# Conv block with a binarized two-layer FFN on one core: another band-load layout, the residual on VectorE, and fp16 parts split over three engines

## The reference

```python
w_sym = (w + rot90(w,1) + rot90(w,2) + rot90(w,3)) * 0.25      # 192 kernels of 7x7
x = x + depthwise_conv(layernorm_over_channels(x), w_sym, pad=3)
t = tokens(x)                                                  # (16, 1024, 192)
h = quant(layernorm(t) @ sign(W1 - mean).T + b1)               # 5 groups along the batch and along the weights' rows
o = quant(gelu(h) @ sign(W2 - mean).T + b2)                    # quant(y) = clip(y * 128 / (max|y| + 1e-5))
x = from_tokens(t + o)
```

## Time and profile before

| | us |
|---|---|
| median of 3 runs | 747.52 |
| the profiled execution | 749.42 |
| its span | 747.5 |

### The profile page before, as it was taken

One profiled execution on the slowest core, in us unless ns is written; L12 is line 12 of the kernel. 1 busy time (PEld: TensorE's weight loads), 2 busy tenths in 40 slices (PEclk: granted clock), 3 DMA queues, 4 the chain that ended last, 5 costly groups with the idle time before them and its releaser, 6 DMA issues.

```text
span 747.5 us, 9920 instructions
## 1 busy us (share of the span) xinstructions
PE 567.7 (76%) x3618; PEld 378.9 (51%) x3618; DVE 481.8 (64%) x1082; ACT 425.7 (57%) x666; POOL 13.7 (2%) x27
## 2 busy tenths in 40 slices
PE   4443379999449798365677888889898898989964
PEld 3443268888348687232233444445455454545543
DVE  1979501010002656859889677799999999988752
ACT  3689600000000040144489887899999999999910
POOL 3001000000000000000000000000000000000000
PEclk9878599999759899578899998999999999999985
DMA  7985167777537474980001010022212131213455
GB/s 184 312 183 139 45 154 180 185 191 169 128 92 181 119 178 103 354 300 0 2 21 43 22 42 22 1 63 65 80 48 85 64 128 65 84 57 114 143 165 157
DMA packets 92438, 87.20 MB, mean 117 GB/s; under 512 B 10153, under 2 KB 75689, under 8 KB 92390
## 3 DMA queue, kind: packets, MB, share of 16 engines
q1 hardware_dynamic: 57040, 69.66, 32.3%
q10 hardware_dynamic: 35350, 16.92, 9.2%
HBM read 62.55 MB, written 23.99 MB: 116 GB/s over the span
## 4 chain that ended last, share of the span: by engine, by line
PE 39%; ACT 25%; DVE 13%; issue 11%; DMA 7%; ACTq 3%; SPq 1%; POOL 0%; POOLq 0%; DVEq 0%
PE bank L876 16%; ACT arena L499 8%; ACT arena L493 6%; PE bank L947 6%; PE bank L865 5%; ACT arena L507 4%; DMA arena<-x 3%; DMA arena<-kz_d 3%; DVE ST L606 2%; ACT arena L516 2%; PE bank L926 2%; ACT arena L479 2%; PE bank L928 2%; PE bank L927 2%; PE bank L912 2%
## 5 line engine op out<-in xcount | busy, mean ns | idle before, releaser
L876 PEld LDWEIGHTS bank<-arena 128*128 128x128 f32 x1152 | 141.7, 199 | 51.4 <-DMA arena<-kz_d 30.1
L876 PE MATMUL bank<-arena 128*128 128x112 f32 (+1 forms) x1152 | 142.3, 282 | 25.1 <-DMA arena<-kz_d 25.1
L493 ACT ACTIVATE arena<-bank,b1s 128x512 f32<-128x512 f32 x180 | 125.4, 700 | 60.7 <-PE bank L928 60.3
L947 PE MATMUL bank<-arena 128*128 128x512 f32 (+1 forms) x360 | 123.5, 440 | 35.4 <-ACT arena L516 35.4
L672 DVE COPY arena<-bank 128x512 f32<-128x512 f32 x24 | 16.6, 691 | 163.5 <-PE bank L876 163.4
L432 ACT ACTIVATE arena<-bank 128x512 f32<-128x512 f32 x24 | 14.3, 595 | 178.9 <-PE bank L876 162.0
L756 DVE TENSOR_TENSOR arena<-arena 128x1024 f16<-128x1024 f32 (+1 forms) x60 | 98.8, 1659 | 24.4 <-ACT arena L507 24.3
L761 DVE TENSOR_REDUCE am<-arena 128x1 f32<-128x3072 f32 x30 | 100.2, 3340 | 0.5 <-ACT arena L493 0.5
L499 ACT ACTIVATE arena<-arena,gm 128x1024 f32<-128x1024 f32 x90 | 100.5, 1167 | 0.0
L926 PE MATMUL bank<-arena 128*128 128x512 f16 x180 | 71.9, 399 | 36.0 <-DVE arena L751 13.9
L507 ACT ACTIVATE arena<-arena 128x1024 f16<-128x1024 f32 (+1 forms) x90 | 82.8, 929 | 0.9 <-PE bank L957 0.9
(11 more groups left out here) (115 smaller groups left out, 657.4 us busy)
## 6 DMA issues: line engine op xcount, KB each, us to landing
arena<-park_d SPq DMA_DIRECT2D x44, 384.0 KB, 3.5
arena<-kz_d SPq DMA_DIRECT2D x96, 96.0 KB, 3.0
arena<-kz_d ACTq DMA_DIRECT2D x96, 96.0 KB, 2.8
park_d<-arena SPq DMA_DIRECT2D x6, 1536.0 KB, 15.0
arena<-x SPq DMA_DIRECT2D x8, 1024.0 KB, 9.5
out<-arena SPq DMA_DIRECT2D x32, 256.0 KB, 2.0
arena<-kz_d SPq DMA_DIRECT2D x96, 64.0 KB, 2.5
arena<-kz_d ACTq DMA_DIRECT2D x96, 64.0 KB, 3.0
```

The lines of the kernel that those rows point to most:

```text
L493: act.activation(yslot(s)[:, 2 * m:2 * m + 2, :], m1p[c % 2][:, :].rearrange("p (h n) -> p h n", h=2), ACT.Identity, bias=b1s[:, m:m + 1], ...
L876: last = t.matmul(ps[:, :, lo:hi], WB[BUFS[u]][:, 1 - db, e, :], xn[:, :, lo + db:hi + db], start=False, stop=(c == CG - 1 and db == -1))
L947: last = t.matmul(o, wt[:, 0:P], src, start=(m == n == 0), stop=(m == MT - 1 and n == 1))
```

## The change

The band table gets another form. `KX[channel pair half, column w, channel, kernel row, w']` is built with 32 copies, stored in four pieces (two DMAs each, interleaved with the third and fourth pair's loads), and read in units of four channels with runs of 896 bytes, all on SP's queue. A buffer holds for each channel 12 blocks of 32 columns, of which seven are written and the rest stay at the zeros that GpSimd writes once; there are two buffers, from unit 3 on three, from unit 24 on four. The rows of a block are in natural order, so `perm` and `by_rows` go. The residual is added by VectorE, which evicts all 48 groups. In the FFN `W2F` goes; all six blocks are fp16 high and low parts. ScalarE makes the high parts of blocks 0 to 2, VectorE those of blocks 3 to 5 in one copy, GpSimd all low parts in six instructions of 512 columns. From step 6 on `normal` and the new `high` stand first in VectorE's step.

```diff
-CG, CU = 4, 2
+CG = 4
+NQ = 3 * RB
+WW = CG * NQ * W
+KW = CG // 2 * KS * W
+KP = 8
-FIRST = 12
-BUFS = [u % 4 if u < FIRST else (4, 5, 0, 1, 2, 3)[(u - FIRST) % 6] for u in range(NCU)]
+THIRD, FOURTH = 3, 24
+BUFS = [(0, 1, 0)[u] if u < THIRD else (2, 1, 0)[(u - THIRD) % 3] if u < FOURTH else (3, 2, 1, 0)[(u - FOURTH) % 4]
+        for u in range(NCG)]
...
+                if k in (2, 3):
+                    for i in range(2 * (k - 2), 2 * (k - 1)):
+                        sp.wait_ge(ker_step, 8 + KP * (i + 1))
+                        for h in range(2):
+                            sp.dma_start(kz_d[:, KP * i:KP * (i + 1), h * KW:(h + 1) * KW],
+                                         KX[h * NCG:(h + 1) * NCG, KP * i:KP * (i + 1)].rearrange("p w s a u -> p w (s a u)")) \
+                                .then_inc(st_ker[i], 16)
+            def load_bands(u):
+                for r in range(RB):
+                    dst = WF[BUFS[u]][r * W:(r + 1) * W].rearrange("p (c q) -> p c q", c=CG)
+                    sp.dma_start(dst[:, :, (r + 1) * W:(r + 1 + KS) * W], kz_d[u].rearrange("w (c q) -> w c q", c=CG)) \
+                        .then_inc(ld_wb[BUFS[u]], 16)
+            for u in range(NCG):
+                sp.wait_ge(blank, 1 if u < THIRD else 2 if u < FOURTH else 3)
+                if user_before(u) >= 0:
+                    sp.wait_ge(conv, user_before(u) + 1)
+                load_bands(u)
...
+            pool.memset(view(R, 2 * WW), 0.0).then_inc(blank, 1)
+            pool.wait_ge(conv, THIRD)
+            pool.memset(WF[2], 0.0).then_inc(blank, 1)
+            pool.wait_ge(conv, FOURTH - 1)
+            pool.memset(WF[3], 0.0).then_inc(blank, 1)
+            def low(u, m0, done):
+                pool.wait_ge(done, u + 1)
+                for m in range(m0, m0 + half):
+                    last = pool.tensor_tensor(out=low_half(u, m, m + 1), in0=yslot(u)[:, 2 * m:2 * m + 2, :],
+                                              in1=hib(u, m, m + 1), op=ALU.subtract)
+                last.then_inc(lo2, 1)
             for s in range(FT + LAGF):
+                if 0 <= s - LAGH < FT:
+                    low(s - LAGH, half, hiV)
                 if 1 <= s <= FT and s % GT == 0:
                     g = s // GT - 1
                     pool.wait_ge(gmx, g + 1)
                     pool.partition_all_reduce(gm[:, 1:2], gm[:, 0:1], P, RMAX).then_inc(gall, 1)
+                if 0 <= s - LAGH < FT:
+                    low(s - LAGH, 0, hiA)
...
-                    if m in (0, 1, 3) and 0 <= k < FT:
-                        high(k, min(m, 2))
+                    if m < 2 and 0 <= k < FT:
+                        high(k, 2 * m, m + 2)
-                    if m >= 4 and 0 <= u < FT:
-                        gelus(u, m - 4)
+                    if m >= 3 and 0 <= u < FT:
+                        gelus(u, m - 3)
-                if 0 <= u < FT:
-                    gelus(u, 2)
...
             for g in range(NCG):
-                if g % 2:
-                    dve.wait_ge(conv, 2 * (g + 1))
-                    dst, src = conv_out_parts(g)
-                    v.tensor_copy(dst, src).then_inc(cev[1], 1)
+                dve.wait_ge(conv, g + 1)
+                dst, src = conv_out_parts(g)
+                v.tensor_tensor(out=dst, in0=src, in1=dst, op=ALU.add).then_inc(cev, 1)
...
+            def high(u):
+                dve.wait_ge(gelu, 3 * (u + 1))
+                if u >= 2:
+                    dve.wait_ge(mm2[1], u - 1)
+                v.tensor_copy(hib(u, MT // 2, MT), yslot(u)[:, MT:2 * MT, :]).then_inc(hiV, 1)
...
+                if s > 5 and s + 2 < FT:
+                    normal(s + 2)
+                if 0 <= s - LAGH < FT:
+                    high(s - LAGH)
...
-                if 0 <= s - LAGH < FT:
-                    low(s - LAGH, 0)
-                if 0 <= s - LAGH < FT:
-                    low(s - LAGH, 1)
...
             def conv_group(g):
                 if g >= 4:
-                    pe.wait_ge(cev[g % 2], (g - 4) // 2 + 1)
-                dst, src = cps[g % 4], X1[:, :, g * CG:(g + 1) * CG]
-                t.matmul(dst[:, :].rearrange("p (c n) -> p n c", c=CG), perm, src, start=True, stop=False)
+                    pe.wait_ge(cev, g - 3)
+                pe.wait_ge(ld_wb[BUFS[g]], 16 * RB * uses(g))
...
             def products(u, m):
-                if m < MF:
-                    return ((W2F, yslot(u)[:, 2 * m:2 * m + 2, :]),)
-                return ((W2T[:, m, :], hib(u, m, m + 1)), (W2T[:, m, :], low_half(u, m, m + 1)))
+                return hib(u, m, m + 1), low_half(u, m, m + 1)
             def lower(u, m):
                 if m == 0:
-                    pe.wait_ge(gelu, 3 * u + 1)
+                    pe.wait_ge(lo2, 2 * u + 2)
```

More of the change, by code:

```diff
@@ L43 @@
 OW = HALF + QTR
-WTN = (3 * HID + MT * C) // 2 + C
-PREP = 15
+WTN = (3 * HID + MT * C) // 2
+PREP = 14
 ARENA = 52544
@@ L240, in var1, with unit_pieces @@
             return VR[:, 2 * NB * (k % 3):2 * NB * (k % 3 + 1)]
[L242 to L247, removed]
+        KER_STEPS = 8 + W + 1
+        def unit_pieces(k):
+            return [i for i in range(W // KP) if i * KP * KW < (k - 1) * 2 * NB * C and (i + 1) * KP * KW > (k - 2) * 2 * NB * C]
         def batch_of(i):
@@ L499, in gelus, with high @@
                 act.activation(y, y, ACT.Gelu, scale=gm[:, 5:6]).then_inc(gelu, 1)
-            def high(u, part):
-                if part == 0 and u >= 2:
+            def high(u, m0, m1):
+                act.wait_ge(gelu, 3 * (u + 1))
+                if u >= 2:
                     act.wait_ge(mm2[1], u - 1)
-                act.wait_ge(gelu, 3 * u + part + 1)
-                m0, m1 = max(MF, 2 * part), 2 * part + 2
-                act.activation(hib(u, m0, m1), yslot(u)[:, 2 * m0:2 * m1, :], ACT.Copy).then_inc(hi2, 1)
+                last = act.activation(hib(u, m0, m1), yslot(u)[:, 2 * m0:2 * m1, :], ACT.Copy)
+                if m1 == MT // 2:
+                    last.then_inc(hiA, 1)
             def result(u, part):
@@ L875, in conv_group @@
                         lo, hi = max(0, -db), min(NB, NB - db)
-                        last = t.matmul(ps[:, :, lo:hi], WB[BUFS[u]][:, 1 - db, e, :], xn[:, :, lo + db:hi + db],
-                                        start=False, stop=(c == CG - 1 and db == -1))
-                    if e == CU - 1:
-                        last.then_inc(conv, 1)
+                        last = t.matmul(ps[:, :, lo:hi], WB[BUFS[g]][:, 1 - db, c, :], xn[:, :, lo + db:hi + db],
+                                        start=(db == 0), stop=(db == -1))
+                last.then_inc(conv, 1)
             for g in range(NCG):
@@ L930, in products @@
             def products(u, m):
[L932 to L934 removed]
+                return hib(u, m, m + 1), low_half(u, m, m + 1)
             def lower(u, m):
                 if m == 0:
[L938 removed]
+                    pe.wait_ge(lo2, 2 * u + 2)
                     if u >= 1:
                         pe.wait_ge(ev2, 2 * u - 1)
[L941 to L944 removed]
                 o = m2a[:, :].rearrange("p (h n) -> p h n", h=2)
[L946 to L947 removed]
+                for n, src in enumerate(products(u, m)):
+                    last = t.matmul(o, W2T[:, m, 0:P], src, start=(m == n == 0), stop=(m == MT - 1 and n == 1))
                 if m == MT - 1:
@@ L954, in upper @@
                 for m in range(MT):
-                    for n, (wt, src) in enumerate(products(u, m)):
+                    for n, src in enumerate(products(u, m)):
                         for e in range(2):
-                            last = t.matmul(m2b[e * C1:(e + 1) * C1, 0:QTR], wt[:, P:C], src[:, e, :],
+                            last = t.matmul(m2b[e * C1:(e + 1) * C1, 0:QTR], W2T[:, m, P:C], src[:, e, :],
                                             start=(m == n == 0), stop=(m == MT - 1 and n == 1))
                 last.then_inc(mm2[1], 1)
-            for e in range(2):
-                pe.wait_ge(cev[e], NCG // 2)
+            pe.wait_ge(cev, NCG)
             for s in range(-2, FT + LAGF):
```

178 lines of the change are left out of this document (57 added, 121 removed).

## The result

The changed kernel takes 779.12 us (median of 4 runs, 777.88 to 781.07) against 748.11 (747.02 to 748.77) for the kernel before: ratio 1.0418, 95% interval 1.0392 to 1.0445. It is slower, where 696 and faster were forecast, and it lies outside the range. The profiled execution took 777.88 with a span of 776.1.

What follows compares the result with a forecast made beforehand. TensorE's band products and permutation were taken to bound the convolution, a chain through ScalarE the FFN. Start +9, convolution -43 and FFN -17 on 749.4 gave 698.4, less 1.9: 696 us; range 662 to 735.

Steps and rivals of the forecast that it cites:

- The start, +9: Start: storing the larger band table delays the later pairs' loads and moves its end by 9 us, bounds 0 and 16.
- The permutation, -42, and bands and evictions that keep up: Convolution: dropping 48 permutations of 0.87 us saves 42 us; groups then take 2.67 us, with loads and evictions fast enough.
- rival B: Convolution: band loads from one queue take 3.3 us per unit and bound it, 723 us in all; chance 0.15.
- The first six groups: Convolution's beginning: with two buffers groups 0 to 5 end near 27 us after the start instead of 16, +11 us.
- Weight loads, +8 with bounds 0 and 20: Convolution: weight loads share some engines with the band loads and slow them, costing 8 us.
- group 24's wait: Convolution: unit 24 waits for its buffer's memset behind group 22, +4 us.
- Weight sums, +7: Convolution, behind group 35: TensorE waits for VectorE's eviction, statistics and weight sums and restarts slowly, +7 us.
- FFN steps of 10.5 us: FFN: steps fall from 11.92 to 10.5 us, with ScalarE as the chain.
- One GpSimd subtraction, 1.3 us: FFN: each 512-column GpSimd subtraction takes 1.3 us, bounds 0.5 and 2.8; six make 7.8 us per step.
- rival A: FFN: GpSimd is the bound, a subtraction taking 1.9 us or more; at 2.0 the kernel takes 766 us; chance 0.08.
- The order in GpSimd's queue costs at each group's end: FFN group ends: the all-reduce stands behind three subtractions, so ScalarE's gelus wait about 2.5 us for the scale, three times.
- The tail, +12 and +3: Tail: eight steps go from 6.46 to 8.0 us, bound by GpSimd, +12 us; the group's end adds +3.

Runs made afterwards that it cites:

- e7: e6 with each of the ten weight loads cut in two (48 + 3 and 32 + 6 partitions): 695.8 us.
- e11: e7 with the weight sums cut into five pairs, one behind each of groups 32 to 36: 689.4 us.
- e1: The changed kernel with a 128x1 GpSimd addition in place of each of the ten all-reduces: 696.7 us, one run.
- e5: The kernel before, with 25 small GpSimd operations of several kinds on scratch memory in its idle stretch under the convolution: 749.9 us.
- e3: The kernel before, with one 128x8 GpSimd subtraction on scratch memory ahead of each of the ten waits for the maxima: 751.4 us, one run.
- e6: The changed kernel with the maxima over partitions made by TensorE and VectorE, their broadcasts placed earlier in TensorE's order: 706.1 us.
- e8: e6 with the ten weight loads uncut but issued two at a time, behind groups 24, 26, 28, 30 and 32: 703.4 us.
- e9: The changed kernel with low parts on VectorE, weight loads cut as in e7, and the high copies of pieces 3 to 5 on GpSimd: 697.3 us.

## Why the prediction was wrong

By its own steps:

- **The start, +9.** 8.9 measured. Right, and by the forecast way: VectorE stood 11.9 us for evictions of late pairs where it had stood 4.7.
- **The permutation, -42, and bands and evictions that keep up.** Right, with evictions 2.68 to 2.69 us apart where TensorE does not wait (groups 3 to 6) against 2.67, +1. Band loads landed in a median of 2.7 us and rival B did not come, though four issues of SP took 2.46 us where 1.85 was forecast. The first six groups end 29.0 us behind the start (27 forecast); the small waits behind them are 0.3 to 1.0 us each, some 2 against 5.
- **Weight loads, +8 with bounds 0 and 20.** Mis-sized. With group 24's wait I had 4 + 8 us; 19 were lost, and e7 gives 10.4 back by cutting the loads. These 7 us are most of why the convolution is -34.7 and not -43; the first groups (+2), the weight sums and their restart (+1), the products (+1) and the small waits (-3) are about the rest.
- **Weight sums, +7.** TensorE stood 5.7 us there, and e11 gives 4.5 to 6.4 back. Right.
- **FFN steps of 10.5 us.** 10.47 to 10.48 within groups, in the changed kernel and in e1. Right, ScalarE sets them.
- **One GpSimd subtraction, 1.3 us.** 1.19 (1.13 apart in a row of three). Right; rival A, that GpSimd's throughput is the bound, did not come. The time landed near rival A's 766 for another reason.
- **"The order in GpSimd's queue costs at each group's end: ... ScalarE's gelus wait about 2.5 us".** This is the step that failed. It counted what stood ahead of the all-reduce in GpSimd's queue, and nothing for going from subtraction to all-reduce and back. Eight of the ten maxima cost GpSimd some 5.9 us ahead of them and 7.0 behind. Of the 103 us of issue time 82 reach the end (779.1 - 696.7), 10 for each of the eight. It also struck twice in each group, since the second layer's maximum has the same form; there I had charged nothing. Without the change of code the price is smaller than my 2.5: in e1 only two of the steps are longer than 10.5, by 1.4 us each.
- **The tail, +12 and +3.** In e1 the last eight steps take 61.4 us, 7.7 a step against 8.0. Near.

Without that one term the sum would have stood: e1 does all of the change except the maxima over partitions and takes 696.7 us, where 696 was forecast. That it agrees to 1 us is luck: two smaller errors cancel in it, the convolution 9.5 us above mine and the FFN 10 below (group ends 2.9 us for 7.5, the tail's steps 2.6 less, and no 3 us at the last group's end).

The rows of the kernel before held a hint that I read as none: GpSimd had memset, affine select, one tensor_scalar and, 276 us of waiting later, all-reduces without a gap. By e5 the first two are neutral and by e3 the last one's load lay under the wait, so those rows could not show a price. One stand of the same look was there, at GpSimd's first affine select:

```profile
10.71 0.28 POOL L343 TENSOR_SCALAR_AFFINE_SELECT identf<-identf 128x128 f32<-128x128 f32 x1 [9.79 <-issue]
```

It was not followed, and what fills it is not shown, but it says that GpSimd can stand for microseconds between two operations with nothing to wait for. A price that cannot appear in a trace is not bounded by it; the chance of rival A (0.08) was far too small for "something on GpSimd other than the subtraction's length".

## What to carry to other kernels

Before giving an engine a second kind of work, list the kinds it will alternate between and measure the change from one to the other with small operations in an idle stretch: here 5.8 to 7.5 us each way between arithmetic and the all-reduce, nothing ahead of copies and memsets. If both kinds are needed, keep the rare one on another engine (about 1 us per maximum by TensorE and VectorE), give GpSimd only neutral work, or make it wait for the rare one long enough that the change is over. To leave the rare operation out is a sound test of such a term: e1 had none of the ten 0.38 us all-reduces, and 82 us went.

## What the runs showed of the hardware

- GpSimd's change from arithmetic to the all-reduce starts while it waits for the next operation's semaphore: VectorE had its answer in 0.55 us where GpSimd had waited 11.6 us or more (e3), and in 6.50 us where the semaphore was there already (the changed kernel).
- Ten loads of 51 or 38 partitions beside a stream of 112 KB band loads cost the kernel 10.4 us more than the same bytes cut at 48 and 32 partitions (e6 against e7), while issuing them two at a time gave 2.7 us (e8).
- GpSimd's 128x512 fp32 to fp16 copy takes 0.6 us in a row of three (1.87) and 784 ns in the mean of e9, against 1191 ns for the subtraction of the same size.
